# A Flamingo block on one core: another order for the first chunk, its weight preparation and the last down tiles

## The reference

```
x = x + tanh(g_xattn) * attention(layernorm(x), ctx, ctx, mask)   # 16 heads of 16
x = x + tanh(g_ffn)   * ffn(layernorm(x))
attention: softmax((q @ k.T) / 4 + mask * -1e9) @ v, then @ Wo + bo
ffn:       h = gelu(qat_lora(x, W_fc));  qat_lora(h, W_proj)
qat_lora(x, W, b, A, B) = x @ quant(W).T + b + 2 * (x @ A.T) @ B.T
quant(W):  scale = max|W| / 127;  clip(round(W / scale), -128, 127) * scale
```

## Time and profile before

| | |
|---|---|
| median of 3 runs | 223.13 us (218.1 to 223.13) |
| the profiled execution | 220.24 us |
| its span, first to last instruction | 218.5 us |
| mean granted PE clock | 0.953 |
| busy: PE, DVE, ACT, POOL | 186.3, 156.5, 116.2, 107.8 us |

### The profile page before, as it was taken

How to read it: one execution, slowest core, us unless ns; L and a number is a source line. 1 busy time by engine, 2 the same in 40 slices (tenths; PEclk the granted TensorE clock), 3 DMA queues, 4 the chain that set the end, 5 groups by cost and what they waited for, 6 DMA issues and landing times.

```text
span 218.5 us, 3162 instructions
## 1 busy us (share of the span) xinstructions
PE 186.3 (85%) x1089; PEld 141.9 (65%) x1089; DVE 156.5 (72%) x305; ACT 116.2 (53%) x199; POOL 107.8 (49%) x138
## 2 busy tenths in 40 slices
PE   1759597979694899999997899999978989899793
PEld 0627473546472798597676775976767749788591
DVE  3659889887836489777967997779479947935422
ACT  3495137787425925674657256746572562447121
POOL 3436679434236358576636681265467800716300
PEclk9999979799969589999999999999999999999799
DMA  5896000000000500000000000000000000000002
GB/s 171 250 268 253 1 4 0 0 1 3 0 0 1 187 8 0 24 26 21 5 24 0 3 0 24 27 23 1 26 0 3 0 27 26 24 24 0 0 27 72
DMA packets 10151, 8.50 MB, mean 39 GB/s; under 512 B 3180, under 2 KB 9864, under 8 KB 10136
## 3 DMA queue, kind: packets, MB, share of 16 engines
q1 hardware_dynamic: 9680, 8.16, 11.3%
q10 hardware_dynamic: 456, 0.14, 0.4%
HBM read 6.20 MB, written 2.10 MB: 38 GB/s over the span
## 4 chain that ended last, share of the span: by engine, by line
PE 67%; DVE 14%; ACT 9%; POOL 4%; issue 3%; DMA 2%; ACTq 1%; DVEq 0%; POOLq 0%
PE ps L1119 13%; PE ps L1099 6%; PE ps L1103 6%; PE ps L1036 6%; PE ps L946 6%; PE ps L1073 6%; PE ps L1046 5%; PE ps L1056 4%; DVE h_lo L755 4%; PE ps L1063 3%; PE ps L938 3%; PE ps L1110 3%; DVE shifted L710 2%; POOL h_hi L326 2%; ACT wfc_sb L598 2%
## 5 line engine op out<-in xcount | busy, mean ns | idle before, releaser
L308 POOL TENSOR_TENSOR shifted<-shifted,row_max 128x512 f32<-128x512 f32 x32 | 35.7, 1128 | 18.8 <-DVE row_max L717 18.8
L1119 PE MATMUL ps<-wprojT,h_hi 128*128 128x288 f32 x128 | 38.2, 319 | 1.5 <-DVE h_lo L755 1.5
L326 POOL TENSOR_SCALAR h_hi<-wfc_sb 128x512 fp32r<-128x512 f32 x32 | 23.3, 734 | 32.4 <-ACT wfc_sb L598 32.4
L755 DVE TENSOR_TENSOR h_lo<-wfc_sb,h_hi 128x512 fp32r<-128x512 f32 x32 | 23.8, 750 | 19.3 <-POOL h_hi L326 19.3
L1119 PE MATMUL ps<-wprojT,h_lo 128*128 128x288 f32 x128 | 36.7, 308 | 0.0
L598 ACT ACTIVATE wfc_sb<-ps,bias_cols,wscale 128x512 f32<-128x512 f32 x32 | 24.3, 778 | 18.3 <-PE ps L1110 17.2
L425 ACT ACTIVATE probsT<-ps 128x512 f32<-128x512 f32 x32 | 18.8, 598 | 23.9 <-PE ps L1046 23.4
L1119 PEld LDWEIGHTS ps<-wprojT,h_hi 128*128 128x128 f32 x128 | 25.8, 201 | 2.5 <-DVE h_lo L755 2.2
L1036 PE MATMUL ps<-k_hi,qT 128*128 128x256 f32 x64 | 20.5, 341 | 7.0 <-DVE shifted L710 4.2
L1119 PEld LDWEIGHTS ps<-wprojT,h_lo 128*128 128x128 f32 x128 | 25.8, 202 | 0.1
L710 DVE TENSOR_TENSOR shifted<-ps,mask_neg 128x512 f32<-128x512 f32 x32 | 21.6, 685 | 4.9 <-PE ps L1036 4.0
(11 more groups left out here) (137 smaller groups left out, 362.8 us busy)
## 6 DMA issues: line engine op xcount, KB each, us to landing
wfc_sb<-in_L_ffn_W_fc SPq DMA_DIRECT2D x1, 1024.0 KB, 7.6
wproj_sb<-in_L_ffn_W_proj SPq DMA_DIRECT2D x1, 1024.0 KB, 8.0
wproj_sb<-in_x SPq DMA_DIRECT2D x2, 512.0 KB, 3.8
out<-x_front SPq DMA_DIRECT2D x8, 128.0 KB, 1.7
out<-wproj_sb SPq DMA_DIRECT2D x8, 128.0 KB, 1.7
x_front<-in_x SPq DMA_DIRECT2D x2, 256.0 KB, 3.4
x_front<-in_x SPq DMA_DIRECT2D x1, 512.0 KB, 4.7
wk_sb<-in_L_xattn_Wk SPq DMA_DIRECT2D x1, 256.0 KB, 4.6
```

Of the source, the lines that this page charges most:

```text
L308: nc.gpsimd.tensor_tensor(shifted[:, slot], shifted[:, slot], row_max[:, slot].unsqueeze(2).broadcast_to([P, HH, KC]), ALU.subtract)\
L326: nc.gpsimd.tensor_scalar(h_hi[:, f], hidden[:, f % HIDDEN_SLOTS], 1.0, 0.0, ALU.mult, ALU.add)\
L755: nc.vector.tensor_tensor(h_lo[:, f], hidden[:, f % HIDDEN_SLOTS], h_hi[:, f].bitcast(F32), ALU.subtract).then_inc(h_split, 1)
L1119: last = nc.tensor.matmul(dst[:, 0:DOWN], h[:, f, t * P:(t + 1) * P], wprojT[:, f], start=(f == 0 and n == 0), stop=(f == FC - 1 and n == ...
```

## The change

- Start: `first_normed`, `first_queries`, `first_queries_high` and `first_queries_low` handle queries 0 of chunk 0 in halves of 256 tokens; the copies of the transposes go from ACT to DVE (`first_normed_transposed`); keys 1 come after the first queries on PE, ACT and DVE; the mask is scaled on POOL, not ACT. POOL's list has the second `first_keys_low` before shift 0. PE runs 8 + 4 idle bf16 products before and after the context's transposes.
- Values: both halves of the keys are made in one product of 128 rows (POOL copies the context twice, `ctx_twice`), the bias is added by a product of one row, and ACT places them, not DVE.
- W_fc: each half is rounded and clipped on POOL, half 0 after shift 5, half 1 after the last shift; the integers lie in the second buffer of normed, and DVE waits for the second wfcT before it applies the second layernorm of chunk 0. bo is added on POOL after shift 3, not after the last shift.
- W_proj: maximum on DVE between the two normalises, scale after `layernorm_apply`, round and clip of both halves on POOL before the rows are added and before the first hidden tile; `unround_wproj` on ACT before tile 0 and after tile 1; PE turns half 0 after up tile 5 and half 1 after tile 7.
- Chunks 1 to 3: `row_maxima(c, 2)` stands before `mask_scores(c, 3)`.
- Tail: all four first halves of the last down tiles, then all second halves.

```diff
-            def round_weights(n, halves, rounded):
+            def round_weights(n, half, w, rounded, clipped):
                 pool.wait_ge(wscale_ready, n + 1)
-                for w in halves:
-                    nc.gpsimd.tensor_scalar(w, w, wscale_inv[:, n:n + 1], ROUNDER, ALU.mult, ALU.add).then_inc(rounded, 1)
+                nc.gpsimd.tensor_scalar(w, w, wscale_inv[:, n:n + 1], ROUNDER, ALU.mult, ALU.add).then_inc(rounded, 1)
+                pool.wait_ge(rounded, half + 1)
+                nc.gpsimd.tensor_scalar(w, w, ROUNDER + QMAX, ROUNDER - QMAX - 1, ALU.min, ALU.max).then_inc(clipped, 1)
...
+            first_keys_low(0)
+            pool.wait_ge(mask_loaded, 16)
+            nc.gpsimd.tensor_scalar(mask_neg[:], mask_neg[:], NEG, 0.0, ALU.mult, ALU.add).then_inc(mask_ready, 1)
+            first_keys_low(1)
 
             for c in range(CHUNKS):
                 for u in range(UNITS):
@@
                     if c == 0 and u == 3:
-                        round_weights(0, wfc_halves, wfc_rounded)
-                if c == 0:
-                    pool.wait_ge(rows_gated, 1)
-                    add_rows(c, bo_gated, x_bo_ready)
+                        pool.wait_ge(rows_gated, 1)
+                        add_rows(c, bo_gated, x_bo_ready)
+                    if c == 0 and u == 5:
+                        round_weights(0, 0, wfc_halves[0], wfc_rounded, wfc_clipped)
...
+                if c == 0:
+                    round_weights(0, 1, wfc_halves[1], wfc_rounded, wfc_clipped)
...
                 if c == 0:
+                    for half in range(2):
+                        round_weights(1, half, wproj_halves[half], wproj_rounded, wproj_clipped)
                     pool.wait_ge(rows_gated, 2)
...
+                if c == 0:
+                    unround_wproj(0)
                 for f in range(FC):
@@
-                    if c == 0 and f in (5, 6):
-                        unround_wproj(f - 5)
+                    if c == 0 and f == 1:
+                        unround_wproj(1)
+                    if c == 0 and f == 6:
+                        read_wprojT(0)
...
+            first_normed_transposed(0)
             dve.wait_ge(consts_ready, 1)
             split_keys(0)
+            first_normed_transposed(1)
             keys_high(0, slice(0, 2))
-            split_keys(1)
-            queries_low(0, 0)
-            keys_high(0, slice(2, 4))
+            first_queries_low(0)
             dve.wait_ge(mask_ready, 1)
             mask_scores(0, 0)
             mask_scores(0, 1)
             row_maxima(0, 0)
+            first_queries_low(1)
+            split_keys(1)
             row_maxima(0, 1)
-            mask_scores(0, 2)
-            queries_low(0, 1)
+            keys_high(0, slice(2, 4))
...
+                if c == 0:
+                    wait_full(dve, ("wfcT", 1))
                 layernorm_apply(1, c, (0, 1), nth(c, 2, 0))
                 layernorm_apply(1, c, (2, 3), nth(c, 2, 1))
+                if c == 0:
+                    weight_scale(1)
...
+            pe.wait_ge(v_zeroed, 1)
+            idle_matmuls(8)
...
                 for f in range(EARLY, FC):
-                    if c == 0 and f == 4:
-                        spread_wmax(1)
                     up_high(c, f)
                     up_low(c, f)
                     up_lora(c, f - EARLY)
+                    if c == 0 and f == 5:
+                        transpose_wproj(0)
+                    if c == 0 and f == 7:
+                        transpose_wproj(1)
...
             for t in range(T):
                 down(LAST, t, 0)
+            for t in range(T):
+                down(LAST, t, 1)
                 if t:
                     turn_t2(LAST, t - 1)
-                down(LAST, t, 1)
-                if t:
-                    finish_down(LAST, t - 1)
+                if t > 1:
+                    finish_down(LAST, t - 2)
             turn_t2(LAST, T - 1)
+            finish_down(LAST, T - 2)
             finish_down(LAST, T - 1)
```

More of the change, by code:

```diff
@@ L46, in bank_sequence @@
         if c == 0:
-            order += [(("wprojT", n), 6 + n) for n in range(2)]
+            order += [(("wprojT", 0), 6), (("wprojT", 1), 3)]
     return order + [(("down", chunks - 1, t), TAIL_BANKS[t]) for t in range(4)]
@@ L66, in flamingo_block @@
     N = T * P
+    HALF = N // 2
     C = S // N
@@ L412, in queries_high, with first_queries_high @@
                                          bias=bq_cols[row:row + HP, m:m + 1]).then_inc(qhi_ready, 1)
+            def first_queries_high(half):
+                key = ("first_q", half)
+                wait_full(act, key)
+                for g in range(2):
+                    row = g * HP
+                    nc.scalar.activation(qT[0:HP, g, half * HALF:(half + 1) * HALF], bank(key)[row:row + HP, 0:HALF],
+                                         ACT.Identity, bias=bq_cols[row:row + HP, 0:1]).then_inc(first_qhi_ready, 1)
             def normalise_input(c, tiles):
@@ L684, in low_a @@
                 dve.sem_inc(freed("aT"), 1)
-            def clip_weights(n, halves, rounded, clipped):
-                dve.wait_ge(rounded, n + 1)
-                nc.vector.tensor_scalar(halves[n], halves[n], ROUNDER + QMAX, ROUNDER - QMAX - 1, ALU.min, ALU.max)\
-                    .then_inc(clipped, 1)
-            def place_values():
-                wait_full(dve, "v")
-                dve.wait_ge(bv_loaded, 16)
-                for e in range(NB):
-                    src = bank("v")[:, e * D:(e + 1) * D].rearrange("p (j i d) -> p j i d", i=2, d=DH)
-                    row = bv_sb[:].rearrange("p (j i d) -> p j i d", i=2, d=DH)
-                    for i in range(2):
-                        keys = slice(i * KC, (i + 1) * KC)
-                        last = nc.vector.tensor_tensor(v_blocks[keys, e, :, i], src[keys, :, i], row[keys, :, i], ALU.add)
-                last.then_inc(v_blocks_ready, 1)
-                dve.wait_ge(v_blocks_ready, 1)
-                dve.sem_inc(freed("v"), 1)
             def mask_scores(c, u):
@@ L913, in _ @@
                 feed_forward(c)
-            for t in range(T):
+            t2_low(LAST, 0)
+            for t in range(1, T):
                 t2_low(LAST, t)
-                gated_ffn(LAST, t)
+                gated_ffn(LAST, t - 1)
+            gated_ffn(LAST, T - 1)
         @block.tensor
@@ L948, in queries, with first_normed, first_queries @@
                 done(last, ("q", c, m))
+            def first_normed(half):
+                key = ("first_xT", half)
+                dst = claim(key)
+                for t in (2 * half, 2 * half + 1):
+                    pe.wait_ge(normed_ready[0], t + 1)
+                    for k in range(KD):
+                        at = k * HALF + t % 2 * P
+                        last = nc.tensor.transpose(dst[:, at:at + P], normed[:, 0, t, k * P:(k + 1) * P], ident[:])
+                done(last, key)
+            def first_queries(half):
+                key = ("first_q", half)
+                wait_read(pe, ("first_xT", half))
+                dst = claim(key)
+                for k in range(KD):
+                    last = nc.tensor.matmul(dst[:, 0:HALF], wq_sb[:, k, 0:P], xnT[:, k, half * HALF:(half + 1) * HALF],
+                                            start=(k == 0), stop=(k == KD - 1))
+                done(last, key)
             def keys(m):
```

178 lines of the change are left out of this document (107 added, 71 removed).

## The result

The changed kernel takes 208.02 us (median of 4 runs, 207.57 to 208.85) against 221.28 for the kernel before beside it (4 runs, 218.1 to 223.13): ratio 0.951, 95% interval 0.944 to 0.958. That ratio leaves out executions over 1.5% above the fastest of their kernel, here two of 223.13, and so compares means of 208.1 and 218.8; the medians in this document are of all executions. The profiled execution took 208.01 us with a span of 206.1.

What follows compares the result with a forecast made beforehand. PE was taken to bound the steady loop, leaving gains only in chunk 0 and the tail. Terms 1.0 + 1.0 + 9.2 + 1.0 - 0.8 + 3.6 = 15.0 took the span from 218.5 to 203.5; forecast 206 us, range 201 to 211.5.

Steps and rivals of the forecast that it cites:

- chunk 0 up to the end of the second normalise: Chunk 0's attention: second normalise ends at 41.8 us instead of 42.82, gain 1.0, bounds -1.5 and 3.0.
- first up stage: Chunk 0's first up products: stage shrinks from 21.16 to 12.0 us, gain 9.2, bounded by 9.6 and 6.7.
- chunk 1's attention: Chunk 1: without PE's stand for the integers the attention takes 31.4 us, gain 1.0, bounds -0.8 and 1.4.
- third maximum, chunks 2 and 3: Attention of chunks 2 and 3: bank 1 held longer, PE's sixth scores wait; cost 0.8 us, bounds 0 and 1.2.
- tail: Last down products: first halves fill PE's wait for the last low part; gain 3.6 us, bounds 2.0 and 4.3.
- Rival (e): Whole kernel slower because clips on POOL are slow; a clip of 8.5 us gives 228 us; chance 0.03.
- Rival (a): First up stage: POOL holds it, weights and rows contended, hidden tiles and wprojT late; stage 14.5, 208.5 us; chance 0.20.
- the last shift is where it was: Chunk 0's attention: POOL's fuller list, from 19.1 us, ends near 35.7, leaving the last shift's time unchanged.
- rival (b): First attention: POOL's full list delays the last shift by 1.5, new DVE wait loses its slack; 209.5 us; chance 0.12.
- the first scores at 13.4: Start of chunk 0: first score product near 13.4 us instead of 15.30, 1.9 earlier, a lead not kept.
- values of full width: Chunk 0, before the first up product: full-width values make 12 PE passes of 16, 0.5 us, under waits.
- idle products: Start of chunk 0: twelve idle products may lift PE's clock, early transposes near 270 ns, worth 0 to 1 us.

Runs made afterwards that it cites:

- Experiment 2: Changed kernel with all of W_proj's preparation (maximum, rounding, clips, copies, turns) put back where it was; median 215.38 us.
- Experiment 1: Changed kernel with the last chunk's down tiles, copies and low parts in the old order, tile by tile; median 211.39 us.
- experiment 6: Changed kernel with POOL's second low keys after shift 0 instead of before it; median 206.18 us.
- experiment 12: Changed kernel with POOL's second low keys after shift 0 and the third maximum again after the fourth mask in chunks 1 to 3; median 206.74 us.
- Experiment 3: Changed kernel without the 8 and 4 idle products at the start; median 207.58 us.
- Experiment 7: Changed kernel with ACT's first read of wprojT after hidden tile 3 instead of tile 6; median 207.71 us.
- Experiment 4: Changed kernel with the third maximum again after the fourth mask in chunks 1 to 3; median 206.71 us.
- Experiments 5: Changed kernel with the values made again in halves of 64 keys, the bias still by a product; median 207.71 us.
- 11: Changed kernel with second low keys after shift 0, values behind scores 7, first half of W_fc after the last shift, old order of third maximum; median 205.88 us.

## Why the prediction came out as it did

The forecast was 206.0 us in a range of 201.0 to 211.5; the kernel takes 208.0. By its terms, each against the profiled execution (predicted, measured, both as gains in us):

| term | predicted | measured | from |
|---|---|---|---|
| chunk 0 up to the end of the second normalise | 1.0 | -0.8 | 42.82 to 43.66 |
| from there to the first up product | 1.0 | 1.2 | 9.44 to 8.23 |
| first up stage | 9.2 | 8.8 | 20.92 to 12.12 |
| chunk 1's attention | 1.0 | 0.1 | 32.53 to 32.43 |
| third maximum, chunks 2 and 3 | -0.8 | -0.7 | 33.09 to 33.45, 30.41 to 30.77 |
| later up stages | 0 | 0.0 | 10.50, 10.52, 10.54 to 10.51, 10.53, 10.49 |
| tail | 3.6 | 3.8 | 17.73 to 13.91 |
| sum | 15.0 | 12.4 | 218.5 to 206.1 |

The span was missed by 2.6 us (203.5 forecast), the time by 2.0. That the second is smaller is luck. The prediction added 0.8, because the median of the kernel before lay above its profiled execution; the median of the changed kernel lies on its own (208.02 and 208.01).

**Right: the first up stage.** The walk came out: POOL's first hidden tile 0.4 us late (0.5 predicted), the stage 12.12 us (12.0), PE without a gap. Experiment 2 shows that the W_proj path alone does nearly all of it (8.4 us). Rival (e) falls with a clip of 1.04 us. Rival (a) falls too: the four operations took 1.12, 1.04, 1.13 and 1.04, not 1.65. (Its own sum has a slip: 0.9 + 6.6 + 2.54 makes POOL free at A + 10.0, not 10.4.) Why they weren't stretched the traces show elsewhere. In the changed kernel's chunk 2, POOL's shifts take 1.42 us beside DVE's low part of a hidden tile and 1.05 without it; start, length, engine, operation, in two stretches:

```profile
112.90 0.68 DVE L795 TENSOR_TENSOR h_lo<-wfc_sb,h_hi 128x512 fp32r<-128x512 f32 x1
...
113.06 1.42 POOL L314 TENSOR_TENSOR shifted<-shifted,row_max 128x512 f32<-128x512 f32 x1 [0.50 <-DVE row_max L757]
...
116.30 1.05 POOL L314 TENSOR_TENSOR shifted<-shifted,row_max 128x512 f32<-128x512 f32 x1 [0.27 <-DVE row_max L757]
```

That low part reads two tensors in SBUF. Beside the four weight operations DVE ran low parts of queries and of x2T, which read one from PSUM. The Trainium skill (SBUF — State Buffer, SBUF: two separate sides) makes just this distinction: DVE holds the shared pair in an operation with two SBUF inputs. The traces agree in direction: 1.42 against 1.05, a stretch of 0.37 us where the two lie together for 0.52. The slow rounding of the kernel before was of this kind. It was the first of the two and not the second, as the prediction has it: by the timeline it took 1.66 us from 64.12, beside a low part of a hidden tile (0.69 us from 64.18), and the second took 1.12. In the prediction I cited the rule without asking which operation of DVE would run beside.

**Right: the tail**, 3.8 us for 3.6, one block and one late copy, as walked through. Experiment 1 adds what the prediction had not worked out: the whole is 2.1 or 4.7 us longer with the old order, from execution to execution, and in the profiled one the clock falls after PE's waits.

**Wrong: "the last shift is where it was".** This is the step that failed. POOL's list began where it was put (19.31, predicted 19.1) and ended at 37.40, not 35.7, where it had ended at 35.62. I summed today's durations, 16.6 us, as if POOL's list alone set the last shift. The trace has 17.09 of work and 1.0 of idle. Of the idle, 0.66 is for maxima that stand on DVE behind the scale of W_fc, for which PE was late at its lower clock. The prediction had no term for that clock: by windows of 1 us it falls between 20 and 21 us now (0.92), between 27 and 28 in the kernel before (0.58). What lies behind the last shift gained what I gave it (7.20 us to the second normalise before, 6.26 now; 0.94 against 1.0). Experiments 6 and 12 both have the second low keys behind shift 0. The last shift ends at 35.64 where the clock held and at 37.14 where it fell, as late as in experiments with the low keys in front. So with the clock down the place in POOL's list is worth nothing. What it is worth by itself with the clock up isn't shown: no profiled run has the low keys in front and the clock held. Half of rival (b) happened, the last shift 1.8 us late, and the other half not: the wait for wfcT kept its slack. PE ends its turn at 47.02 (46.41 + 0.61) and the reciprocal deviation that DVE needs comes at 48.37 (47.66 + 0.71), 1.35 us later (1.3 predicted).

**Wrong, but harmless: the first scores at 13.4.** They start at 14.69 here and at 13.9 to 14.0 in nine of the experiments. The load of W_k took 6.4 us to land in the changed kernel's profiled execution, 4.6 in that of before and 3.7 to 6.0 in the experiments, and PE does half of the transposes ahead of the keys. Experiment 3, which starts its scores 0.8 us earlier, reaches the first up product only 0.3 earlier (51.55).

**Wrong: chunk 1's gain.** Its clock is 1.00 and PE's work 30.79 us, as predicted, but the stage didn't shrink, since PE now waits 1.64 us there, of which the timeline puts 0.82 down to the late copy of wprojT and 0.69 to DVE's mask. Experiment 7 takes the first wait away and nothing is gained. Experiment 4 takes 0.25 us off DVE's row of masks and maxima, with the wait for wprojT as it was, and the stage gets 0.36 shorter (32.07). So the chain through DVE sets the stage's length rather than PE's work; that follows from these two experiments and wasn't tested by itself. I had read PE's 32.39 of 32.43 as PE's bound. With the old order of maxima full clock would have brought 0.5 (32.53 to 32.07), and the new order, which I charged with nothing in chunk 1, takes 0.36 of it back.

**Wrong mechanism, right size by luck: the third maximum.** I charged a bank held longer, 0.8 us in chunks 2 and 3, and they lost 0.7. PE's waits are the same in both orders; the cost is DVE's own pace in dependent operations. It falls in all three chunks, 0.31 to 0.36 us each, 1.0 in all.

**Wrong: values of full width** save 0.5 us, and **idle products** bring transposes to 270 ns. The values go from 1.95 us for 16 narrow products to 3.3 (29.25 to 32.52) with the bias. Experiments 5 and 3 show that neither width nor idle products move the time.

**Open.** Why the clock falls in one execution of a kernel and holds in another, with the same instructions up to that point (experiments 6 and 12 have 0.71 and 0.74 us of PE work in the window before). Open too is why PE's busy time in chunk 1 grows when wprojT comes earlier (experiment 7). The versions of experiments 6 and 11 are 1.8 and 2.1 us faster than the changed kernel by their medians; no choice between them is supported.

## What to carry to other kernels

When work is moved onto an engine that had gaps, write its whole list in order with start times, and ask what stands in front of the first item of the critical chain: here one low part placed ahead of shift 0 left PE idle for 2.15 us, its clock fell, and a transpose that PE then made late (the spread of W_fc's maximum) held DVE and POOL. Moved back, it gained 1.8 us in experiment 6, where the clock held, and nothing up to the last shift in experiment 12, where the clock fell all the same. Before pricing contention between two engines, look at which operation runs beside which, and whether it reads two tensors in SBUF. Cut the stages of two kernels at the same instruction before comparing them: a cut 0.16 us off hides nearly half of the 0.36 us that the third maximum costs a chunk. And a stage that looks full on one engine at a lowered clock is no proof of its bound: a second engine may be right behind it.

## What the runs showed of the hardware

- POOL clips 128 x 1024 fp32 (minimum and maximum) in 1.04 us and rounds it (multiply and add) in 1.12.
- Products of 64 columns of the array, in pairs for the upper and the lower rows of the result, take no longer than half as many of 128: 8 take 1.08 us, 4 of 128 columns 1.03. The pairs must run side by side.
- A product of a single row is not cheap: two (1 x 128 by 1 x 256) take 0.69 us, four of 128 rows and the same width 1.03.
- On DVE (128 x 512 fp32, 0.68 us each) an operation that reads what the one before wrote starts 0.71 us after it, an independent one 0.60.
- POOL's shift takes 1.42 us beside a DVE operation with both inputs in SBUF, 1.05 beside a mask, which reads one from PSUM.
- Twelve bf16 products ahead of the first transposes, 2.95 us of PE work between 1.5 and 5.4 us, don't bring them from 1.11 us for four to the 0.60 that four take later. The Trainium skill (TensorE: Matmul & The Clock Gate, What's actually happening) says that activity releases the throttle; these products didn't, and the durations, as long as those at a granted clock of 0.50 (1.11 us for four transposes at 24.07), are of 1.2 GHz while the clock column says 1.00.
- With the same instructions, the clock fell to 0.50 in one execution (experiment 12) and not in another (experiment 6), in a wait of 1.31 us of PE; the same stage took 26.92 and 25.45 us.
